# DLRM tower on one core: table batches first, 256-column one-hot products, row numbers spread by TensorE

## The reference

```python
e = jnp.stack([tbl_0[ids[:, 0]], ..., tbl_31[ids[:, 31]]], axis=1)   # [512, 32, 256] f32
dots = jnp.einsum('bnd,bmd->bnm', e, e)                              # 32 x 32 for each sample
z = dots[:, iu, ju]                                                  # upper triangle, 496 values
h = jnp.concatenate([z, dense_ctx], axis=1)                          # 496 + 16 = 512
h = jnp.maximum(h @ W_top1 + b_top1, 0.0)                            # 512 x 512
h = jnp.maximum(h @ W_top2 + b_top2, 0.0)                            # 512 x 256
y = h @ W_top3                                                       # 256 x 1
```

## Time and profile before

| what | value |
|---|---|
| median of the 3 runs shown | 183.59 us (181.79 to 184.43) |
| the profiled execution | 181.27 us |
| its span, first to last instruction | 179.2 us |
| busy in it: TensorE / VectorE / ScalarE / GpSimd | 152.4 / 92.9 / 71.2 / 122.0 us |
| granted TensorE clock over the span | 1.000 |

### The profile page before, as it was taken

One profiled execution on the slowest core, in us unless ns is written; L12 is line 12 of the kernel. 1 busy time (PEld: TensorE's weight loads), 2 busy tenths in 40 slices (PEclk: granted clock), 3 DMA queues, 4 the chain that ended last, 5 costly groups with the idle time before them and its releaser, 6 DMA issues.

```text
span 179.2 us, 3427 instructions
## 1 busy us (share of the span) xinstructions
PE 152.4 (85%) x1278; PEld 144.6 (81%) x1278; DVE 92.9 (52%) x257; ACT 71.2 (40%) x189; POOL 122.0 (68%) x144
## 2 busy tenths in 40 slices
PE   0321698989999999999879999899699999699994
PEld 0100697989999999999779998799599999599893
DVE  3700139328855942432947497473738864554701
ACT  2010025135632740425607286472816623632520
POOL 3777377776877787777777777777777777742700
DMA  1389999999333433433333343433334333330000
GB/s 29 97 176 191 334 323 319 362 341 310 106 95 84 117 86 95 119 100 109 102 106 99 106 116 92 117 102 109 106 99 119 90 117 95 115 88 4 0 0 0
DMA packets 12272, 23.19 MB, mean 129 GB/s; under 512 B 2598, under 2 KB 7744, under 8 KB 12129
## 3 DMA queue, kind: packets, MB, share of 16 engines
q0 software_dynamic: 5760, 15.74, 29.9%
q1 hardware_dynamic: 6497, 7.25, 14.5%
HBM read 22.98 MB, written 0.00 MB: 128 GB/s over the span
## 4 chain that ended last, share of the span: by engine, by line
POOL 43%; issue 23%; DMA 16%; PE 14%; DVE 2%; ACT 1%; POOLq 0%; ACTq 0%; DVEq 0%
POOL rows L328 43%; DMA rows<-in_table,row_number 14%; PE gram_ps L550 6%; PE xt_ps L524 3%; PE mlp_ps L620 2%; DMA ids_sb<-in_ids 1%; PE gram_ps L612 1%; DVE z L320 1%; ACT h_sb L486 1%; PE hot_ps L564 1%; DVE slots L388 1%; PE mlp_ps L630 1%; PE mlp_ps L612 1%; PE xt_ps L612 0%; PE hot_ps L620 0%
## 5 line engine op out<-in xcount | busy, mean ns | idle before, releaser
L328 POOL DMA_INDIRECT rows<-in_table,row_number x64 | 61.1, 955 | 23.9 <-issue 17.4
L328 POOL DMA_INDIRECT rows<-in_table,hot_number x56 | 56.0, 1000 | 17.1 <-issue 14.9
L524 PE MATMUL xt_ps<-identity,rows 128*128 128x128 f32 x238 | 40.8, 288 | 20.6 <-DMA rows<-in_table,row_number 17.6
L524 PEld LDWEIGHTS xt_ps<-identity,rows 128*128 128x128 f32 x238 | 28.6, 147 | 25.6 <-issue 12.9
L564 PE MATMUL hot_ps<-one_hot,hot_table 128*128 128x128 f32 (+2 forms) x272 | 34.8, 275 | 0.0
L550 PE MATMUL gram_ps<-xt 128*128 128x128 f32 x248 | 33.6, 285 | 0.0
L564 PEld LDWEIGHTS hot_ps<-one_hot,hot_table 128*128 128x128 f32 (+2 forms) x272 | 32.4, 192 | 0.3 <-issue 0.2
L550 PE MATMUL gram_ps<-hot_xt 128*128 128x128 f32 x256 | 32.5, 275 | 0.0
L320 DVE COPY z<-slots 32x32 f32<-32x32 f32 x133 | 30.9, 233 | 2.1
L550 PEld LDWEIGHTS gram_ps<-xt 128*128 128x128 f32 x248 | 31.4, 201 | 0.2 <-issue 0.2
L550 PEld LDWEIGHTS gram_ps<-hot_xt 128*128 128x128 f32 x256 | 30.5, 192 | 0.0
(11 more groups left out here) (45 smaller groups left out, 66.4 us busy)
## 6 DMA issues: line engine op xcount, KB each, us to landing
hot_table<-in_table SPq DMA_DIRECT2D x3, 896.0 KB
hot_table<-in_table SPq DMA_DIRECT2D x1, 1152.0 KB
ids_bc<-in_ids SPq DMA_DIRECT2D x1, 1032.0 KB, 10.7
rows<-in_table,row_number POOLq DMA_INDIRECT x64, 3.0
w1z_sb<-in_w1z SPq DMA_DIRECT2D x1, 1024.0 KB, 10.3
rows<-in_table,hot_number POOLq DMA_INDIRECT x56, 2.8
...
```

The lines of the kernel that those rows point to most:

```text
L328: nc.gpsimd.indirect_dma_start(rows[:, n % RING, :], None, table, bass.IndirectOffsetOnAxis(ap=numbers, axis=0),).then_inc(rows_landed[n % ...
L524: done = nc.tensor.transpose(tile_ps(n)[:, k, :], rows[:, n % RING, k * P:(k + 1) * P], identity[:])
```

## The change

- `HOT` becomes (0, 1). The order of units is `ORDER` = 8, 0 to 7, 9 to 15: steps 0 to 3 are four plain pairs of batch 2, steps 4 to 31 are the 28 pairs of both table batches, steps 32 to 59 are the other 28 plain pairs.
- A one-hot product has 256 columns, the same field of both batches at once: 68 products in place of 136, each counted as 4 passes. They begin at step 3 and end at step 17 (3 a step in steps 3 to 5, 5 a step in 6 to 16, 4 in 17). Fields alternate between `hot_ps` and `mlp_ps`. `mark` makes two compares for each field, one for each batch; those of fields 0 and 1 stand at p = 1, of field 2 at p = 8, of field 3 at p = 11. `copy_hot` copies one field of both batches, at 8, 11, 14, 18.
- The DMA of `ids_bc` goes. VectorE converts the row numbers to f32 and multiplies them by the identity, so that each partition holds its own (`hot_ids_apart`, 128 x 1024), TensorE multiplies that by a matrix of ones (`spread_ids`, behind the transposes of pair 0), and ScalarE copies the 128 x 1024 result from `gram_ps1` to `ids_bc`.
- Gram pairs of the table batches wait until all four fields are done: none in steps 6 to 18, then two a step in steps 19 to 27. Planned passes, a 256-column product counted as 4: 24 a step in steps 3 to 16, 20 in step 17, 4 in step 18, 20 or 22 in steps 19 to 53 (24 in steps 35 and 46), then 20, 16, 12, 12, 12 in steps 54 to 58. `TURN` is 28, 39, 48.
- Step 58 has gram pair 61 alone behind the last transposes, and gram pair 62 and the last one follow the loop.
- VectorE's opening turns the row numbers batch by batch, with 32 small copies of half the width in place of 16, has the 128 x 1024 product ahead of them, and clears the two tiles last. `XT_RING` is 12.
- SP: table 0 at count 1, table 1 at 3, table 2 at 6, table 3 at 9, `w1z`, context, biases, `w2` at 12.

```diff
-XT_RING = 8
+XT_RING = 12
...
-HOT = (1, 2)
+HOT = (0, 1)
...
+FIRST = BT // UNIT * (HOT[-1] + 1)
+ORDER = [FIRST] + list(range(FIRST)) + list(range(FIRST + 1, UNITS))
+PAIR = []
+for u in ORDER:
+    b, v = divmod(u, BT // UNIT)
+    if b not in HOT:
+        PAIR += [(b, UNIT // 2 * v + t) for t in range(UNIT // 2)]
+    elif v % 2 == 0:
+        PAIR += [(b, v // 2, i) for i in range(GATHERS)]
...
+def product_pair(i):
+    return UNIT // 2 * ORDER[i // (UNIT // 2)] + i % (UNIT // 2)
...
 def gram_of(p):
...
+    return next(i for i in range(GRAM_PAIRS) if product_pair(i) == BT // 2 * b + t)
...
+def pairs_before(i):
+    b, t = divmod(product_pair(i), BT // 2)
...
+SHARE = 24
+HOT_FROM = 3
+HOT_LIST = [(f, k, c) for f in range(HF) for k in range(KD) for c in range(CHUNKS[f])]
+HOT_PASSES = 2 * len(HOT)
...
+def can_multiply(i, step):
+    b = product_pair(i) // (BT // 2)
+    if b in HOT and HOT_ENDS.get(HF - 1, step) + 1 >= step:
+        return False
+    return pairs_before(i) + (step < PAIRS - 8) <= step
...
+    due = []
+    for i in range(at, min(at + 2, GRAM_PAIRS)):
+        if not can_multiply(i, step) or 4 + 8 * (len(due) + 1) + layer_passes(step) > SHARE:
+            break
+        due.append(i)
+    GRAMS.append(due)
+    TURN += [step + APART for i in due if product_pair(i) % (BT // 2) == BT // 2 - 1 and product_pair(i) < GRAM_PAIRS - 1]
+    left = HOT_LIST[sum(map(len, HOTS)):]
+    many = max(0, SHARE - 4 - 8 * len(due) - layer_passes(step)) // HOT_PASSES if step >= HOT_FROM else 0
+    HOTS.append(left[:many])
+    for field, k, c in HOTS[step]:
+        HOT_BEGINS.setdefault(field, step)
+        if (k, c) == (KD - 1, CHUNKS[field] - 1):
+            HOT_ENDS[field] = step
+ENDED = [[i // 4 for i in GRAMS[step] if i % 4 == 3] for step in range(PAIRS)]
 LAST_UNIT = UNITS - 1
...
+        hot_ids = sbuf("hot_ids", [P, HOT_TILES])
+        hot_ids_apart = sbuf("hot_ids_apart", [P, J, HF, HOT_TILES])
+        ids_bc = sbuf("ids_bc", [P, J, HF, HOT_TILES])
+        ones = sbuf("ones", [P, P])
+        row_in_chunk = sbuf("row_in_chunk", [P, MOST], I32)
+        table_row = sbuf("table_row", [P, MOST])
         hot_table = sbuf("hot_table", [P, sum(CHUNKS), D])
-        one_hot = sbuf("one_hot", [P, 2, MOST, J, F])
+        one_hot = sbuf("one_hot", [P, 2, MOST, len(HOT), J, F])
...
+        spread_ps = gram_ps[1][:].rearrange("p g j f -> p (g j f)")
...
+        def field_ps(f):
+            return mlp_ps[:].rearrange("p (k h) n -> p k (h n)", k=KD) if f % 2 else hot_ps[:]
...
-            sp.dma_start(ids_bc[:], ids.rearrange("(j f) t -> j f t", f=F)[None, :, HOT_FIELD:F, :]
-                         .broadcast_to(ids_bc.shape)).then_inc(ids_bc_loaded, 16)
             load_table(0)
             sp.wait_ge(transposed, 3)
             load_table(1)
+            sp.wait_ge(transposed, 6)
+            load_table(2)
+            sp.wait_ge(transposed, 9)
+            load_table(3)
+            sp.wait_ge(transposed, 12)
+            sp.dma_start(w1z_sb[:], w1z).then_inc(w1_loaded, 16)
             sp.wait_ge(ctx_cleared, 1)
             sp.dma_start(ctx_sb[0:CTX, :], ctx_t).then_inc(ctx_loaded, 16)
             sp.dma_start(w1c_sb[0:CTX, :], w1c).then_inc(ctx_loaded, 16)
...
+                if p == 0 or p == PLAIN[UNIT // 2]:
+                    pool.wait_ge(numbered, 1 if p == 0 else 3)
...
-                if b in HOT:
-                    pool.wait_ge(hot_numbered, 1)
+                if b in HOT and PAIR[p][1:] == (0, 0):
+                    pool.wait_ge(hot_numbered, HOT.index(b) + 1)
...
+            number(slice(UNIT * FIRST, UNIT * (FIRST + 1)))
+            number(slice(0, UNIT * FIRST))
+            nc.vector.memset(ones[:], 1.0)
+            nc.vector.tensor_copy(hot_ids[:], ids_sb[:, BT * HOT[0]:BT * (HOT[-1] + 1)]).then_inc(ids_apart, 1)
+            dve.wait_ge(identity_loaded, 16)
+            dve.wait_ge(ids_apart, 1)
+            own = identity[:].rearrange("p (j f) -> p j f", j=J)[:, :, HOT_FIELD:F]
+            nc.vector.tensor_tensor(hot_ids_apart[:], hot_ids[:, None, None, :].broadcast_to(hot_ids_apart.shape),
+                                    own[:, :, :, None].broadcast_to(hot_ids_apart.shape), ALU.mult).then_inc(ids_apart, 1)
+            dve.wait_ge(rows_in_chunk, 1)
+            nc.vector.tensor_copy(table_row[:], row_in_chunk[:]).then_inc(ids_apart, 1)
+            dve.wait_ge(numbered, 2)
+            for h, b in enumerate(HOT):
+                nc.vector.transpose(row_number_t[:, h, :], row_number[:, BT * b:BT * (b + 1)]).then_inc(turned, 1)
+            for h in range(len(HOT)):
+                dve.wait_ge(turned, h + 1)
+                for a in range(A):
+                    for j in range(J):
+                        done = nc.vector.tensor_copy(hot_number[F * a:F * a + F, h, j, :],
+                                                     row_number_t[F * j:F * j + F, h, a:HOT_FIELD:A])
+                done.then_inc(hot_numbered, 1)
+            number(slice(UNIT * (FIRST + 1), TILES))
             nc.vector.memset(ctx_sb[:], 0.0)
             nc.vector.memset(w1c_sb[:], 0.0).then_inc(ctx_cleared, 1)
...
+            def mark(f):
...
+                if f == 0:
+                    dve.wait_ge(ids_bc_ready, 1)
+                    dve.wait_ge(ids_apart, 3)
+                if f >= 2:
+                    dve.wait_ge(hot_done, f - 1)
+                for h in range(len(HOT)):
+                    to = one_hot[:, f % 2, 0:c, h]
+                    numbers = ids_bc[:, :, f, BT * h:BT * (h + 1)]
+                    done = nc.vector.tensor_tensor(to, numbers[:, None].broadcast_to(to.shape),
+                                                   table_row[:, 0:c, None, None].broadcast_to(to.shape), ALU.is_equal)
+                done.then_inc(one_hot_ready, 1)
...
+            def copy_hot(f):
...
+                act.wait_ge(hot_done, f + 1)
+                nc.scalar.copy(hot_xt[:, :, :, :, :, HOT_FIELD + f].rearrange("p h j k s -> p (h j) k s"),
+                               field_ps(f).rearrange("p k (g s) -> p g k s", s=F)).then_inc(hot_copied, 1)
+            act.wait_ge(ids_spread, 1)
+            nc.scalar.copy(ids_bc[:].rearrange("p j f t -> p (j f t)"), spread_ps).then_inc(ids_bc_ready, 1)
...
+                for f in range(HF):
+                    if p == HOT_ENDS[f] + 1:
+                        copy_hot(f)
...
+            def hot(f, k, c):
                 if k == 0 and c == 0:
-                    if h == 0:
-                        pe.wait_ge(hot_loaded[f], 32)
-                    pe.wait_ge(one_hot_ready, field + 1)
-                    if field >= 2 and field % 2 == 0:
...
+                    pe.wait_ge(hot_loaded[f], 32)
+                    pe.wait_ge(one_hot_ready, f + 1)
+                    if f >= 2:
+                        pe.wait_ge(hot_copied, f - 1)
                 r = chunk_rows(f, c)
-                done = nc.tensor.matmul(hot_ps[:, field % 2, :, k, :], hot_table[0:r, CHUNK_AT[f] + c, k * P:(k + 1) * P],
-                                        one_hot[0:r, field % 2, c], start=(c == 0), stop=(c == CHUNKS[f] - 1))
+                done = nc.tensor.matmul(field_ps(f)[:, k, :], hot_table[0:r, CHUNK_AT[f] + c, k * P:(k + 1) * P],
+                                        one_hot[0:r, f % 2, c].rearrange("p h j s -> p (h j s)"),
+                                        start=(c == 0), stop=(c == CHUNKS[f] - 1))
...
+            def spread_ids():
+                pe.wait_ge(ids_apart, 2)
+                numbers = hot_ids_apart[:].rearrange("p j f t -> p (j f t)")
+                for half in range(2):
+                    done = nc.tensor.matmul(spread_ps[:, half * B:(half + 1) * B], ones[:], numbers[:, half * B:(half + 1) * B],
+                                            start=True, stop=True)
+                done.then_inc(ids_spread, 1)
...
-                    if q % UNIT == 0:
+                    if q % 4 == 0:
                         pe.wait_ge(xt_ready[0], last // 2 + 1)
                         pe.wait_ge(xt_ready[1], (last + 1) // 2)
-                        pe.wait_ge(hot_copied, HF // 2 * (HOT.index(q // (BT // 2)) + 1))
+                        pe.wait_ge(hot_copied, HF)
...
+                if i == UNIT // 2:
+                    pe.wait_ge(ids_bc_ready, 1)
...
+                    if batch:
+                        pe.wait_ge(y_ready, batch)
+                    else:
+                        pe.wait_ge(hot_copied, HF)
...
+                units = max(map(ORDER.index, range(BT // UNIT * batch, BT // UNIT * (batch + 1)))) + 1 - (batch == LAST)
...
+                if p == 0:
+                    spread_ids()
```

127 lines of the change are left out of this document (30 added, 97 removed).

## The result

The changed kernel took 174.8 us, the median of four runs (173.83 to 175.82), against 182.69 for four runs of the kernel before (181.32 to 184.43). The ratio is 0.9593, with a 95% interval of 0.9508 to 0.9677. The predicted sign and range held; the predicted time of 178.2 was 3.4 us too long. Its profiled execution took 174.69 us, with a span of 172.8.

The account below looks back on a forecast made before the run. Bound: GpSimd's gather pace to 158 us, then TensorE's backlog, then a fixed tail. Last gather 152.0 + 0.3 + 3.9 = 156.2, with the tail 5.35 us off 181.27: 175.9, plus the offset 178.2; range 174 to 184.

Parts of the forecast that it names:

- Term 1: GpSimd's waits at the gather ring: 2.6 us become about 0.3, as the `ids_bc` transfer goes.
- the cover: Slack in the opening between TensorE's transposes of pair 4, about 20 us, and GpSimd's need, 23.2 or later: 3 us.
- Term 2: Gathers held while VectorE compares run: 3.5 us stay about 3.9, ends 2.5 and 5.5 us.
- what else: Remaining causes that lengthen gathers, besides the compares and the opening's new product: 0.5 us.
- that rule: Skill page's inference that two-input VectorE instructions leave descriptor generation alone: lengthened gathers near 0, time about 174.8 us.
- Term 3: Work behind the last gather: 21.05 us become about 17.7, by 28 fewer passes (3.1) and less backlog (0.3).
- the level ends: Behind the last gather, GpSimd's cells end at 8.5 us and VectorE's at 8.8: level, nothing taken off.
- The offset: Profiled execution lies 2.3 us under the median of 183.59; kept, taking 175.9 to 178.2.
- Rival C: Better than the sum: less varied early traffic removes the 2.3 us offset, or few gathers are held; 175, chance 0.15.
- A: TensorE too late in the table stretch: each us beyond the cover costs one, 181.5 with 3.3; chance 0.20.
- B: TensorE's clock falls to half rate at the end and stays: 10.2 us more, 188.4; chance 0.06.
- D: A new wait at steps 18 and 19, for all four fields copied, stops the ring: 183.6, chance 0.06.

Follow-up runs that it names:

- experiment 1: Changed kernel with the row numbers sent to all partitions by the `ids_bc` DMA again, without multiplication, spreading and copy; 177.39 us, ratio 0.9761.
- experiment 5: Changed kernel with no gram pairs in steps 55 to 57, so 48 passes behind the last transposes in place of 24; 180.14 us, ratio 0.9906.
- experiment 6: experiment 5 with 12 transposes of the identity, whose results nothing reads, added in each of steps 55 to 58; 179.28 us, ratio 0.987.
- experiment 7: Changed kernel with gram pair 61 ahead of the last transposes in place of behind them; 175.17 us, ratio 0.9645.
- experiment 8: Changed kernel without the 14 warming transposes ahead of the last layers; 175.47 us, ratio 0.9657.
- experiment 9: Changed kernel with gram pairs 61, 62 and tile 126's product ahead of the last tile's transposes, and ten GpSimd cells moved to VectorE and ScalarE; 173.72 us.
- experiment 2: Changed kernel with each long compare of two SBUF tiles replaced by short one-input compares, one per 128 table rows; 171.83 us, ratio 0.945.
- experiment 11: experiment 10 with the last unit's cells shared 6, 5 and 5 by VectorE, ScalarE and GpSimd, not 7, 6 and 3; 171.02 us, ratio 0.9392.
- experiment 10: Changed kernel with the edits of experiment 9 and experiment 2 together; 171.93 us, ratio 0.9421.
- experiment 12: experiment 11 with 4 one-hot products in place of 5 in each odd step from 7 on; 173.97 us, ratio 0.9556.
- experiment 3: Changed kernel with field 1's compares moved from p = 1 to p = 3, two blocks of two in place of one of four; 174.26 us, ratio 0.9592.

## Why the prediction came out as it did

**The bound, and the parts that go.** Right. GpSimd's even pace, what is lost on it, and the work behind the last gather account for the whole gain: 3.07 + 3.33 us of span. By cause: the ring waits 2.6, of which experiment 1 brings back 2.2, the passes behind the last landing 3.1 and the backlog's remainder 0.2, and held gathers about 0.4 (3.5 less 3.1).

**Term 1, ring waits, 2.6 to 0.3.** The cause was right, and the 0.3 was not needed: 0.0. The steps of the cover: VectorE's 32 small copies took 6.57 us (6.3 at most said) and its opening ended at 12.64 (12.8), TensorE's spreading took 3.62 us (3.4), ScalarE's copy 1.01 (1.1), the compares 4.61 (4.7). Pair 4's transposes began at 21.20 and 22.33 and not at 20, the first behind eight gram passes and six table products which I had not counted, the second behind rows that landed 6.8 us behind their gather's start, a gather that had itself been held. But the two held gathers had moved GpSimd's need for them as well, from 23.2 to 25.28, so the cover was 2.5 us, and nothing was lost. The wide passes cost by their columns, as taken, and a step of 24 passes came out at 2.60 us, not 2.67.

**Term 2, lengthened gathers, 3.5 to 3.9: the term that came out lower.** The last gather at 155.08 less the undisturbed 152.0 leaves 3.1. Point by point: the block of four cost 0.96 + 1.01 = 1.97 us (1.7 said, 1.1 to 2.2); the new product in the opening nothing (0.15), since the first gather's 0.18 stands before too; field 3's block 0.69 + 0.15 (0.9); field 2's 0.15 where I had an average of 0.6; "what else" only that 0.18 where I had 0.5. A held gather asks again after 0.82 + 0.30 = 1.12 us, not 1.25. An average was the wrong thing to expect of a phase: in experiments 5 to 9, which leave that stretch as it is, the gap between two gathers there was 2.03 to 2.30 us, so field 2's block cost 0.8 to 1.05, and the gathers' excess came to 3.2 to 4.1 us in all. The 3.9 thus lies inside what this stretch costs from run to run, and the 3.1 of the profiled execution below it by the phase of one block.

The Trainium skill, page "SBUF — State Buffer", section "Who interferes with whom", infers that an instruction with two SBUF inputs leaves descriptor generation alone. The rows at 13.31 and 15.52 decide against that inference for a gather that reads its row numbers from SBUF: 1.90 and 1.96 us beside compares with two SBUF inputs, 0.946 undisturbed, and experiment 2 takes the loss away with the compares. They don't tell which part of the gather is held, the reading of its row numbers or the making of descriptors. The 174.8 us which that rule gave were reached in another way, by luck.

**Term 3, behind the last gather, 21.05 to 17.7.** Measured 17.72. The passes' price held in experiment 6, the level ends in experiment 7.

**The offset: the step that failed.** The sum gave 175.9 for a profiled execution; it took 174.69, and the 1.2 us are term 2 (0.8), term 1 (0.3) and 0.2 less around the span (174.69 less 172.8 in place of 181.27 less 179.2), with 0.1 back in the tail. On top I kept the 2.3 us by which the profiled execution of before, 181.27, lay under the median of three. After the change the two lie 0.1 apart. Of four runs of before the median is 182.69, so the profiled one had come out low in a spread of 3 us. Rival C gave less varied early traffic as the reason. Experiment 1 speaks against that: with `ids_bc` back its runs spread by only 0.24 us, those of the change by 2.0. It speaks against the phase of the holds too, as it has 3.5 us of them; experiment 2, without holds, spreads by 0.33, and experiment 11, also without, by 1.4. What goes with a good part of the spread is the clock of each run. In experiments 6, 7, 8, 10 and 11 every run at 0.98 took longer than every run at 0.99 (in 12 not, nor does experiment 3 fit), and all four of experiment 1 stand at 1.000. Of the kernel before, in the series of experiments 9 to 11, the runs at 1.000 took 181.23 and 181.97 us, three of those at 0.991 took 182.74 to 183.03 and the fourth 185.55; its profiled execution had 1.000. The traces show where such a loss can lie (0.50 for longer in experiment 10's opening than in experiment 2's). That this made the 2.3 us is argued and not shown: the runs behind the median of three have no clock on record, and the four runs of the change spread by 2.0 us at 0.99 each. So the step that failed is known, an offset kept without a reason that would survive the change, and its cause stays open.

**The rivals.** A did not happen: no ring wait above the usual. It was the next limit all the same, by the 2.60 us a step, once TensorE enters the stretch late: experiment 10 shows its price, experiment 2 the same steps without it, and experiment 12 what evading it costs. B did not happen either: the last transposes took 0.41 us and the layers' passes 1.06 for eight. Its mechanism exists (experiment 5), from lighter steps than the change leaves. C gave the time that was measured, and in part by its own reasons: the offset went and fewer gathers were held, but the less varied traffic that it gave for the first isn't borne out. D did not happen: the gram pairs of the table batches waited 0.4 us in all.

**Granted clock.** The Trainium skill, page "TensorE: Matmul & The Clock Gate", section "What's actually happening", has the rate set by how busy TensorE has recently been. The rows of before could not show the way back to the slow rate. The kernel after does in its opening (0.50 from 16.0 to 19.4 us, eight passes in 1.92), and so does experiment 5 (40 passes in 6.64 us); experiment 8 does not, with 2.07 us of idleness. The printed clock is no proof of full rate at the start: it reads 1.00 up to 12.5 us, where the four passes of 512 columns took 3.62 us.
